# Moving the last product of a normalisation factor from the vector engine to pool

## The reference

```python
def _L0_conv_ref(x, W, b):
    u = jnp.mean(x, axis=1, keepdims=True)
    var = jnp.var(x, axis=1, keepdims=True, ddof=1)
    s = jnp.sqrt(var)
    n_x = (x - u) / (s + EPS)
    n_x = jnp.einsum('bchw,oc->bohw', n_x, W) + b[None, :, None, None]
    return x * n_x
...
x = x + _L0_conv_ref(_gn(x), L0_conv_W, L0_conv_b)
```

## Time and profile before

| what | value |
|---|---|
| median of 3 runs | 1894.35 us (1892.35 to 1896.38) |
| the profiled execution | 1890.62 us |
| its span, first to last instruction | 1888.8 us |
| busy, share of the span | PE 90%, DVE 91%, ACT 77%, POOL 77% |
| chain that ended last | PE 68%, DVE 18%, issue 6%, DMA 3% |

### The profile page before, as it was taken

The page is one execution under the profiler, slowest core; times in us unless marked ns, Lnnn a source line. Parts: engine busy times, 40 slices in busy tenths (PEclk is TensorE's granted clock), DMA queues, the critical chain, the costliest instruction groups (busy, mean ns, idle before and its releaser), DMA issues.

```text
span 1888.8 us, 67606 instructions
## 1 busy us (share of the span) xinstructions
PE 1699.3 (90%) x28706; PEld 920.7 (49%) x28706; DVE 1727.5 (91%) x2120; ACT 1446.4 (77%) x2498; POOL 1458.4 (77%) x1684
## 2 busy tenths in 40 slices
PE   0079998999989999999999999899999999899998
PEld 0045554555545555455555555455545555455553
DVE  5669999999999999999999999999999999988887
ACT  5589886888868986798869889688877898644442
POOL 0068787888878887888878787787877888788885
PEclk9989999999999999999999999999999999999999
DMA  9979999999999999999999999899999999854775
GB/s 375 407 285 375 375 373 327 390 394 391 364 339 406 375 396 342 344 407 382 383 323 393 400 386 381 314 402 386 397 349 340 416 373 397 290 205 189 276 264 221
DMA packets 183036, 667.33 MB, mean 353 GB/s; under 512 B 20560, under 2 KB 20944, under 8 KB 182736
## 3 DMA queue, kind: packets, MB, share of 16 engines
q1 hardware_dynamic: 109008, 394.54, 56.9%
q10 hardware_dynamic: 73728, 268.47, 35.4%
HBM read 394.49 MB, written 268.44 MB: 351 GB/s over the span
## 4 chain that ended last, share of the span: by engine, by line
PE 68%; DVE 18%; issue 6%; DMA 3%; SPq 2%; ACT 2%; POOL 1%; POOLq 0%; ACTq 0%; DVEq 0%
PE proj_ps L731 40%; PE sums_ps L719 15%; PE factor_ps L705 12%; DVE scaled L629 5%; DVE bn L673 4%; DVE bn L674 4%; DMA tiles<-x 3%; SPq L410 2%; DVE tiles L642 1%; DMA out<-tiles 1%; DVE gn L583 1%; ACT unused L511 1%; ACT squares L526 0%; DVE gn L587 0%; POOL tiles L454 0%
## 5 line engine op out<-in xcount | busy, mean ns | idle before, releaser
L731 PE MATMUL proj_ps<-scaled,w_t 128*32 128x512 f32 x8192 | 985.9, 599 | 0.1
L454 POOL TENSOR_SCALAR tiles<-tiles,columns_sb 128x1024 f32<-128x1024 f32 x512 | 576.9, 1127 | 257.4 <-DVE tiles L642 254.4
L642 DVE SCALAR_TENSOR_TENSOR tiles<-proj_ps,columns_sb,tiles 128x1024 f32<-128x1024 f32 x512 | 643.3, 1257 | 69.1 <-PE proj_ps L731 67.5
L511 ACT ACTIVATE unused<-tiles,bn 128x1024 uint8<-128x1024 f32 x560 | 635.2, 1134 | 0.0
L443 POOL TENSOR_SCALAR tiles<-tiles,columns_sb 128x1024 f32<-128x1024 f32 x512 | 620.4, 1212 | 12.9 <-DMA tiles<-x 11.7
L629 DVE TENSOR_TENSOR scaled<-tiles,factor_ps 128x1024 f32<-128x1024 f32 x512 | 619.0, 1209 | 7.2 <-PE factor_ps L705 2.1
L526 ACT ACTIVATE squares<-tiles 128x1024 f32<-128x1024 f32 x512 | 537.8, 1050 | 81.3 <-POOL tiles L443 37.0
L719 PEld LDWEIGHTS sums_ps<-tiles,const_sb 128*32 128x32 f32 x8192 | 245.8, 111 | 316.3 <-issue 265.2
L731 PEld LDWEIGHTS proj_ps<-scaled,w_t 128*32 128x32 f32 x8192 | 213.6, 109 | 360.8 <-issue 306.8
L705 PE MATMUL factor_ps<-pieces,pick_sb 128*128 128x128 bf16 x4096 | 318.1, 221 | 77.2 <-DVE scaled L629 72.5
L719 PE MATMUL sums_ps<-tiles,const_sb 128*32 128x128 f32 x8192 | 320.6, 275 | 11.7 <-ACT squares L526 11.7
(11 more groups left out here) (56 smaller groups left out, 782.3 us busy)
## 6 DMA issues: line engine op xcount, KB each, us to landing
tiles<-x SPq DMA_DIRECT2D x752, 512.0 KB, 8.6
out<-tiles ACTq DMA_DIRECT2D x512, 512.0 KB, 7.1
const_sb<-const SPq DMA_DIRECT2D x1, 85.5 KB, 1.9
scaled<-w SPq DMA_DIRECT2D x1, 64.0 KB, 2.0
scaled<-ident SPq DMA_DIRECT2D x1, 64.0 KB, 1.8
pick_sb<-pick SPq DMA_DIRECT2D x1, 8.0 KB, 2.0
columns_sb<-bias SPq DMA_DIRECT2D x1, 0.5 KB, 2.1
```

Source lines behind the costliest of these rows:

```text
L454: nc.gpsimd.tensor_scalar(place(s), place(s), 1.0, out_shift[:, 0:1], ALU.mult, ALU.add).then_inc(finished, 1)
L511: nc.scalar.activation(unused[:, which, :], data, (ACT.Identity, ACT.Square)[which], bias=pivot_of(of), scale=-1.0, accum_out=act_sums[:, ...
L642: nc.vector.scalar_tensor_tensor(out=place(s), in0=proj_ps[:, s % 2, :], scalar=gate_shift[:, 0:1], in1=place(s), op0=ALU.add, op1=ALU.mul ...
L731: mm = nc.tensor.matmul(proj_ps[q:q + 32, s % 2, h:h + BANK], w_t[:, q:q + 32], scaled[:, s % 2, h:h + BANK], start=True, stop=True)
```

## The change

The last product of the factor, L664 on VectorE in step `LAG_FIT`, is taken out. In its place pool gets two operations directly behind its own two products, in step `LAG_ROOT`: `miss - 2` in place, and the product of that with `approx` into `factor`. Each waits on a semaphore for the operation before it. `factor_done`, for which ACT's first rounding waits, now comes from pool. VectorE no longer waits for `miss_squared`.

```diff
@@ -461,6 +462,10 @@
                 nc.gpsimd.tensor_tensor(miss[:, :], miss[:, :], approx[:, :], ALU.mult).then_inc(miss_scaled, 1)
                 pool.wait_ge(miss_scaled, done)
                 nc.gpsimd.tensor_tensor(miss[:, :], miss[:, :], approx[:, :], ALU.mult).then_inc(miss_squared, 1)
+                pool.wait_ge(miss_squared, done)
+                nc.gpsimd.tensor_scalar(miss[:, :], miss[:, :], 1.0, -2.0, ALU.mult, ALU.add).then_inc(miss_shifted, 1)
+                pool.wait_ge(miss_shifted, done)
+                nc.gpsimd.tensor_tensor(factor[:, :], miss[:, :], approx[:, :], ALU.mult).then_inc(factor_done, 1)
 
             def split_first(done):
 
@@ -658,11 +663,6 @@
                     if (ready := set_behind(step, LAG_ROOT, b, own, before)) is not None:
                         dve.wait_ge(root_eps_done, ready)
                         nc.vector.reciprocal(approx[:, :], approx[:, :]).then_inc(approx_done, 1)
-                    if (ready := set_behind(step, LAG_FIT, b, own, before)) is not None:
-
-                        dve.wait_ge(miss_squared, ready)
-                        nc.vector.scalar_tensor_tensor(out=factor[:, :], in0=miss[:, :], scalar=-2.0, in1=approx[:, :],
-                                                       op0=ALU.add, op1=ALU.mult).then_inc(factor_done, 1)
                     gate()
```

More of the change, by code:

```diff
@@ L299, in norm_gate_kernel @@
         miss_squared = sem("miss_squared")
+        miss_shifted = sem("miss_shifted")
         factor_done = sem("factor_done")
```

## The result

| | median us | lowest to highest | runs |
|---|---|---|---|
| before | 1892.77 | 1891.36 to 1896.38 | 6 |
| changed | 1910.11 | 1907.55 to 1916.64 | 6 |

The ratio of changed to before is 1.0092, with a 95% interval of 1.0075 to 1.011. The change makes the kernel 17.3 us slower. The forecast was +17.1.

A forecast was written before the change was run, and what follows sets the result against it. It took VectorE's chain to bound two-slot sets and TensorE one-slot sets. Terms 17.3, 0.9 and 0.9 sum to 19.1 us, less 2 for loads: 1894.35 + 17.1 = 1911.5 us, range 1900 to 1924.

The forecast's parts named there:

- The price of the addition: Pool's two new operations with handovers push pool back by 0.93 us a set, from 0.81 to 1.08.
- Value of the removal in the ordinary sets: Taking L664 off VectorE, 59.5 us in all, is worth 0 because VectorE's gate waits for TensorE anyway.
- Two-slot sets: Sets with four batch-norm instructions in one step: spread 0.49 us late, swallowed by 0.82 us of TensorE stall; cost 0.
- The sign named for it: After the change, sets with four batch-norm instructions in one step should still be 4.10 + 3 x 3.28 = 13.94 us long.
- One-slot sets: TensorE-bound sets with two batch-norm instructions in one step: each pays 0.51 us, 34 of them, 17.3 us.
- the first batch: Its first TensorE-bound set has no spare time but the handover, so it pays 0.9 us.
- ACT's push: ACT's second rounding waits for L468, its next squares come 0.9 us later; valued at 0.
- Group-norm steps: L468 idles 0.80 us there; a push of 0.93 leaves 0.13 on the chain, x 7 = 0.9 us.
- Last batch: No statistics are left and spare time is 1.09 us, so the 0.93 us delay fits; cost 0.
- Relief by loads: Pool waits 11.7 us for loads; a later TensorE lets loads catch up, taking back 2 us (0 to 6).
- Counts: TensorE's waits for pieces some 90, about 45 us; scaling wait shrunk by the two-slot half; VectorE's gate wait above 100.
- The rule weighed: VectorE operations with two SBUF inputs and GpSimd operations exclude each other; removal frees VectorE, supporting the faster rival, chance 0.07.

The follow-up runs named there:

- e1: Kernel before with L664 taken out and nothing added, pool's second product written straight into the factor: 1887.5 us, ratio 0.9959.
- s2: Changed kernel with pool's order new (both remainders before the finish) and VectorE's statistics laid over two steps of each four: 1858.2 us, ratio to before 0.9798.
- d1: Kernel before plus one unused pool product ahead of pool's finish, VectorE's product kept: 1910.1 us, ratio 1.0075.
- d2: Kernel before plus two unused pool operations (shift and product) ahead of pool's finish, VectorE's product kept: 1935.1 us, ratio 1.0209.
- d4: Kernel before plus two unused pool operations, placed behind pool's finish, VectorE's product kept: 1916.2 us, ratio 1.0114.
- o1: Changed kernel with pool's order first remainder, norm, second remainder, finish: 1888.4 us, ratio to before 0.9969.
- o2: Kernel before with pool's order first remainder, norm, second remainder, finish: 1894.5 us, ratio 1.0003.
- s4: Kernel before with both remainders ahead of pool's finish and VectorE's statistics laid over two steps of each four: 1866.4 us, ratio 0.9858.
- d3: Kernel before plus three unused pool operations ahead of pool's finish, VectorE's product kept: 1963.8 us, ratio 1.0359.
- s3: Changed kernel, pool's order as it was, with VectorE's statistics laid over two steps of each four: 1885.0 us, ratio to before 0.996.

## Why the prediction was right, point by point

- *The price of the addition*: 0.93 us expected, 0.94 measured. The far rows of the shift (188 ns for one column, 1127 for 1024) had given 305 ns; it is 300.
- *Value of the removal in the ordinary sets, 0*: right (e1, 178.0 against 178.0). Outside them it is worth some 8 us by the medians (4.5 in the profiles), which the sum didn't have.
- *Two-slot sets swallow the delay*: right, 3.91 + 3.47 = 7.38 = 3.28 + 4.10 in the lines above. The sign named for it, two-slot sets still 13.94 long, did not come true as it stands, and doesn't test the mechanism: from spread to spread they now run from 13.8 to 14.3, because the lateness of the next set's first spread counts in, and that spread comes 0.72 us late at step 11.
- *One-slot sets pay 0.51*: right in kind, and the size came out between 0.47 and 0.72. In a typical batch the five late spreads measure 0.72, 0.69, 0.47, 0.50 and 0.47 (2.85 us, where 5 x 0.51 = 2.55 stood). At step 11 there was less spare time before (0.25 us, where the one row read had 0.47). In the first batch, where nothing but the handover was to spare, it is 0.72 and not 0.9. At step 23 a part comes over ACT: VectorE's reciprocal, which pool's products wait for, stands still there for 0.63 us waiting for ACT's addition, where it had no wait before (16.3 us in 23 places in all, 7.4 in 11 before). Of ACT's push I had said 0.
- *Group-norm steps, 0.9*: the idle time of 0.80 us ahead of the first remainder (L468, now L473) at step 62 is used up, as said. How much that costs can't be read apart from the rest of the end stretches. One thing there had no term in the sum: the spread at step 59 comes late by 7.6 us in the seven end stretches together, where it was 3.4 before.
- *Last batch, 0*: right, 208.4 against 208.5.
- *Relief by loads, -2*: pool's waits for loads went from 11.7 us in 12 places to 9.2 in 9, so such a relief exists; how much of these 2.5 us TensorE felt, no run shows. s2 moves 406 GB/s in a stretch (560 to 700 us) in which before moved 394, so 394 is not the most that the loads can do.
- *Counts*: TensorE's wait for pieces 46.3 us in 98 places (45 in some 90 forecast), the wait for the scaling down by 30.5 (by "as much" as the half in two-slot sets), the gate's wait 99.1 ("above 100").
- *The rule weighed* was treated too lightly. I used the port's exclusion only as a point for a faster kernel. What it does is in d1 and d2: had the product stayed while pool got as much more ahead of the finish, it would have cost some 19 us (d2 against d4). The change removed the operation that would have been hit.

So the mechanism was right, and that the total came out within a microsecond was luck. The two new operations cost some 25 us where 19.1 was forecast (the changed kernel against e1), and the removal gave back 8 where 0 was forecast, with 2 for the loads. These errors stand against each other. The ordinary stretches carry 17.4 us of the profile's 26.0 and the medians differ by 17.3, so in a typical run the end stretches must about cancel. Which of their parts do so isn't settled: each kernel has one profile, and they vary by 3 us from batch to batch.

## What to carry to other kernels

Price an operation that moves to another engine by what stands behind it in that engine's queue: find the next consumer on the bounding engine, subtract its spare time, and only what is left counts, in those stages in which nothing else waits later. Idle time of the receiving engine says little (pool had 254 us of it and the change still cost 17), and its place does: behind or ahead of the piece that is waited for. What the relief of an engine is worth has to be read with the addition out of the way: here the same move cost 17 us, gave 6 with another order in pool's queue (o1 against o2), and 8 with the statistics spread as well (s2 against s4).

## What the runs showed of the hardware

**An exclusion that moves.** The VectorE product with two SBUF inputs took 448 ns in the mean when pool's finish came where it does in d4, 465 before, 696 in d2 and 862 in d1. Wherever it took over 0.32 us (531 times in the profiles of before and d1 to d4), it ended 0.13 to 0.15 us after the pool operation that was under way when it started. What it meets decides the price: in d1 the finish of 1.12 us nearly always (113 of 122 holds), in d2 in some half (53 of 101, and an extra operation in 44), and in d3 mostly (75 of 89) the extra product of 0.46 us that now stands where the finish was. So of d1, d2 and d3 the last has the shortest hold, 453 ns, and still the longest time; there TensorE waits 103.3 us for pieces, where d2 has 44.4.

**TensorE's clock after the group-norm steps.** In five of the seven end stretches of the changed kernel's profile TensorE runs a stretch at a lower granted clock. The table by stretch (busy us of each engine, then granted clock, DMA share, GB/s):

```profile
300.00:313.00 13.00, 11.16 (x181) 6.05 (x184) 11.79 (x21) 4.87 (x8) 9.59 (x13) 1.00 0.95 330
313.00:317.00 4.00, 2.16 (x48) 1.28 (x41) 3.13 (x10) 1.53 (x4) 3.26 (x5) 1.00 0.75 256
317.00:320.20 3.20, 3.20 (x32) 1.21 (x33) 2.00 (x3) 1.04 (x1) 2.25 (x2) 0.70 1.02 371
```

and TensorE's timeline there:

```profile
316.80 0.61 PE L705 MATMUL factor_ps<-pieces,pick_sb 128*128 128x128 bf16 x8 [1.84 <-DVE scaled L634]
317.34 2.79 PE L731 MATMUL proj_ps<-scaled,w_t 128*32 128x512 f32 x16
...
321.75 0.62 PE L705 MATMUL factor_ps<-pieces,pick_sb 128*128 128x128 bf16 x8
```

After 1.84 us of waiting the 16 matmuls take 2.79 us instead of 1.92, and the step 4.95. In the kernel before, the same place has a wait of 1.73 and a step of 3.26. Mean granted clock 0.70 means that a part of the stretch ran at 1.2 instead of 2.4 GHz. Leaving out the start and the end of the program, a projection of over 2.3 us is found once in the profile of before, 5 times in the changed kernel's, 4 times in o1 and d4, 5 in d2, 6 in d1, 7 in d3 and not once in s3. Each lies in an end stretch, at steps 59 to 63. If each costs as much as this one (4.95 - 3.28 = 1.67 us), the four more make 6.7 of the 8.7 us by which the changed kernel's end stretches are longer in its profile, and the five more of d1 make 8.4 of its 10.7. In d1 this isn't the profiled run alone: its five runs have a mean granted clock of 0.989 to 0.991, and the runs of the kernel before beside them 0.992 to 0.997. In the changed kernel it is: its other five runs have 0.995 to 0.999. Over the 42 runs of the kernel before beside the experiments, 0.001 less of granted clock goes with about 1.3 us more. What decides whether the clock falls at these steps isn't shown: o1 has four such places and is faster than before.
